# Four graph layers on one core: part of the first chunk's row sums moves from TensorE to VectorE, and the work between layers is put in another order

## The reference

```python
def gat(h, W, a):                       # layers 0 and 1; 2 and 3 have other ways to u, v
    Wh = h @ W
    e = leaky_relu((Wh @ a1)[:, None] + (Wh @ a2)[None, :], 0.2)
    att = softmax(where(adj > 0, e, -9e15), axis=1)
    return elu(att @ Wh)

h = relu(layernorm(x)); x = x + gat(h, W0, a0)
h = relu(layernorm(x)); x = x + gat(h, W1, a1)
h0 = relu(layernorm(x))
h1 = 0.2 * h0 + 0.8 * layer(h0, W2[0]); h2 = 0.2 * h0 + 0.8 * layer(h1, W2[1])
x = x + concat([h0, h1, h2]) @ mlp_w + mlp_b
h = relu(layernorm(x)); n = normalize(centre(h))
A = adj * softmax((n @ w_k) @ (n @ w_q).T / sqrt(8)); A = A / A.sum(-1)
x = x + (A + A @ A / 2 + A^4 / 6) @ h
```

## Time and profile before

| what | value |
|---|---|
| median of 3 runs | 585.03 us (584.64 to 595.99) |
| the profiled execution's own time | 580.28 us |
| its span, first to last instruction | 578.4 us |
| mean granted TensorE clock | 0.988 of full speed |
| TensorE busy | 529.5 us, 92% of the span |
| VectorE busy | 380.3 us, 66% |
| ScalarE busy | 263.3 us, 46% |

### The profile page before, as it was taken

The page is one execution under the profiler, slowest core; times in us unless marked ns, Lnnn a source line. Parts: engine busy times, 40 slices in busy tenths (PEclk is TensorE's granted clock), DMA queues, the critical chain, the costliest instruction groups (busy, mean ns, idle before and its releaser), DMA issues.

```text
span 578.4 us, 7918 instructions
## 1 busy us (share of the span) xinstructions
PE 529.5 (92%) x3300; PEld 202.4 (35%) x3300; DVE 380.3 (66%) x551; ACT 263.3 (46%) x297; POOL 30.2 (5%) x32
## 2 busy tenths in 40 slices
PE   6888987998998998998888999999889999999997
PEld 5422222343223343323233223245334344333332
DVE  4888689548979637989765989637977983100000
ACT  3479964534665543665543755444234772000000
POOL 3300000211000100000100000021100000000000
PEclk9879999999999999999999999999999999999999
DMA  8977000000000000000000000000000000000000
GB/s 309 409 280 275 4 1 1 0 2 1 1 0 1 2 0 2 1 1 0 1 1 2 0 2 1 0 1 1 1 1 1 0 1 2 0 1 1 0 19 18
DMA packets 5635, 19.43 MB, mean 34 GB/s; under 512 B 608, under 2 KB 608, under 8 KB 5600
## 3 DMA queue, kind: packets, MB, share of 16 engines
q1 hardware_dynamic: 5600, 18.93, 8.9%
HBM read 18.40 MB, written 0.52 MB: 33 GB/s over the span
## 4 chain that ended last, share of the span: by engine, by line
PE 63%; DVE 23%; ACT 6%; issue 4%; DMA 3%; POOL 1%; SPq 0%; DVEq 0%; ACTq 0%
PE PROD L793 11%; DVE X L1361 10%; PE X L1062 10%; PE PROD L1062 9%; PE X L785 7%; PE S L813 6%; ACT big L471 4%; DMA big<-in_adjT 3%; PE X L1053 2%; DVE tops L1625 2%; DVE big L1373 2%; PE M L648 1%; DVE nadj L1475 1%; PE M L747 1%; DVE big L1370 1%
## 5 line engine op out<-in xcount | busy, mean ns | idle before, releaser
L471 ACT ACTIVATE big<-X,v 128x1024 f32<-128x1024 f32 x128 | 141.6, 1114 | 100.5 <-PE X L785 100.1
L1361 DVE SCALAR_TENSOR_TENSOR X<-wB,v,aB 128x1024 f32<-128x1024 f32 x128 | 163.4, 1293 | 27.6 <-ACT big L471 26.3
L793 PE MATMUL PROD<-big,Wh 128*64 128x512 f32 x512 | 134.3, 605 | 1.9 <-ACT big L471 1.7
L785 PE MATMUL X<-nadj,bigI 128*64 128x512 bf16 x512 | 77.9, 383 | 19.6 <-DVE X L1361 19.3
L785 PEld LDWEIGHTS X<-nadj,bigI 128*64 128x64 bf16 x512 | 25.3, 109 | 102.3 <-DVE X L1361 73.2
L813 PE MATMUL S<-big,onesf 128*32 128x512 f32 x400 | 53.3, 604 | 2.4 <-DVE big L1373 2.4
L793 PEld LDWEIGHTS PROD<-big,Wh 128*64 128x64 f32 x512 | 31.1, 136 | 52.2 <-issue 30.3
L1062 PE MATMUL PROD<-big,Wh 128*64 128x512 f32 x128 | 30.6, 594 | 0.0
L528 ACT ACTIVATE big<-nadj 128x1024 fp8e4<-128x1024 bf16 x26 | 26.3, 1053 | 9.0 <-DVE nadj L1475 9.0
L398 POOL TENSOR_TENSOR rr<-var,mhalf 128x8 f32<-128x8 f32 x8 | 14.5, 1818 | 298.7 <-DVE var L1222 298.7
L1062 PE MATMUL X<-big,Wh 128*64 128x512 f32 x128 | 28.6, 595 | 0.0
(11 more groups left out here) (307 smaller groups left out, 597.2 us busy)
## 6 DMA issues: line engine op xcount, KB each, us to landing
big<-in_adjT SPq DMA_DIRECT2D x28, 512.0 KB, 7.5
aB<-in_adjT SPq DMA_DIRECT2D x4, 512.0 KB, 7.5
cst<-in_cst SPq DMA_DIRECT2D x1, 537.0 KB, 7.5
x<-in_xT SPq DMA_DIRECT2D x1, 512.0 KB, 3.7
out<-x SPq DMA_DIRECT2D x2, 256.0 KB, 2.0
late<-in_late SPq DMA_DIRECT2D x1, 272.5 KB, 5.8
cst<-in_cst SPq DMA_DIRECT2D x1, 263.0 KB, 2.8
```

The costliest lines, as they stand in the source:

```text
L471: act.activation(prob[:, t % U, :], X[t % 2][:], ACT.Exp, bias=v2[l % 2][:, k:k + 1]).then_inc(p_ready, 1)
L785: last = pe.matmul(X[t % 2][feat(side), hh * BANK:(hh + 1) * BANK], bigI[:, feat(side)], nadj[:, k, half_cols(c, hh)], start=False, stop=T ...
L793: last = pe.matmul(PROD[c][feat(hh), :], Wh[l % 2][:, k, :], prob[:, t % U, hh * BANK:(hh + 1) * BANK], start=k == 0, stop=k == NB - 1)
L1361: dve.scalar_tensor_tensor(X[t % 2][:], wB[:, cols(c)], v8[l % 2][:, k:k + 1], aB[:, cols(c)], ALU.max, ALU.add).then_inc(x_written, 1)
```

## The change

Six things change.

1. **First chunk.** `added(0)` is now (4, 5, 8, 9, 12). VectorE adds these tiles into h0, which is not yet used for its own purpose: 4 and 5 after the exponents of tile 7, 8 after tile 10, 9 after 11, 12 after 14. `sums` of the pairs (4, 5) and (8, 9) are not issued; the sums of (12, 13) read h0 in place of tile 12.
2. **Loads and early products.** Blocks 18 to 21 of `adj` go to slots 0 to 3, the others of the second half to other slots than before. Two `repeat` products each follow the level products of blocks 9, 10, 12 and 13; six in place of four follow `w_broadcast(1)`.
3. **End of the first chunk.** The level products of blocks 14 and 15 go ahead of the sums of tiles 10 and 11, and `shift_products(0, 2, 4)` goes ahead of the products of tiles 12 and 13. In the last pair the next chunk's masks go ahead of the sums.
4. **From layer 0 to 1 and from 1 to 2.** The first chunk's `features` on TensorE go from in front of the last sums to behind `centre`; on VectorE its features, rows, levels and row parts go behind `clip`. The early levels go behind all of this in one piece, and `w_broadcast` goes behind the next layer's top levels, in front of the shift products. In layer 2 `root_broadcast(0)` goes behind the shift products, and `input_rows(0)` on VectorE behind the exponents of tile 1.
5. **The terms of h0 and h1 in the `mlp`.** They leave `mlp(c)` for `skip_terms(c)`, into banks of their own: chunk 0 at the end of layer 2, chunk 1 at the start of layer 3, where 8 `repeat` products stand in place of 17. `skip_rows(c)` adds them and the bias to x; `mlp_rows` becomes a plain addition.
6. **From layer 2 to 3.** `features(7)` goes ahead of the last 20 early level products; three `repeat` products stand in place of four.

```diff
+        ADD_FIRST = {7: (5,), 10: (8,), 11: (9,), 14: (12,)}
         ADDS = 4
-        SLOT_OF = [n % SLOTS for n in range(NB)] + [(7, 8, 4, 5, 6)[j % 5] for j in range(NB)]
+        SLOT_OF = [n % SLOTS for n in range(NB)] + [(7, 8, 0, 1, 2, 3, 4, 5, 6, 7, 8, 4, 5, 6, 7, 8)[j] for j in range(NB)]
...
             if c_all == 0:
-                return ()
+                return (4, 5, 8, 9, 12)
...
+        def sum_buffer(c_all):
+            return acc[c_all % NCH] if c_all else h0[:].rearrange("p c n -> p (c n)")
...
+        def skip_bank(c):
+            return (X[1][:, BANK:CH], M[:])[c]
...
             def top_levels(l):
...
-                pe.wait_ge(wB_ready, 2 * (2 * l + 1))
+                if l in (0, 3):
+                    pe.wait_ge(wB_ready, 2 * (2 * l + 1))
                 for jb in range(CB if l else 0, NB):
                     if l == 0:
                         chunk_levels(0, jb)
+                        if jb in (9, 10, 12, 13):
+                            repeat(X[1][:, BANK:CH], 2)
                         continue
...
-                if l == 2:
-                    root_broadcast(0)
-                elif l:
+                if l in (1, 2):
+                    w_broadcast(2 * l)
+                if l:
                     repeat(X[0], 4)
...
                 shift_products(l, 0, 4 if l else 2)
+                if l == 2:
+                    root_broadcast(0)
...
             def mlp(c):
                 n = NCH * 3 + c
-                pe.wait_ge(ld_late, 16)
                 pe.wait_ge(p_copied, n + 1)
-                for k, src in enumerate((h0, h1)):
-                    pe.matmul(EB[c][:], mw[:, k, :], src[:, c, :], start=k == 0, stop=False)
                 pe.wait_ge(t_ready, n + 1)
-                pe.matmul(EB[c][:], mw[:, 2, :], tb, start=False, stop=False)
+                pe.matmul(EB[c][:], mw[:, 2, :], tb, start=True, stop=False)
...
+            def skip_terms(c):
+
+                pe.wait_ge(ld_late, 16)
+                pe.wait_ge(h0_ready, c + 1)
+                pe.wait_ge(h_ready, c + 1)
+                pe.matmul(skip_bank(c), mw[:, 0, :], h0[:, c, :], start=True, stop=False)
+                pe.matmul(skip_bank(c), mw[:, 1, :], h1[:, c, :], start=False, stop=True).then_inc(skip_psum, 1)
...
                 if l < 2:
                     centre_old(2 * l + 3)
-                    early_levels(l + 1, 0, 2)
                     centre(2 * l + 3)
-                    w_broadcast(2 * l + 2)
+                    features(2 * l + 2)
                     variances(2 * l + 3)
-                    early_levels(l + 1, 2, 4)
                     features(2 * l + 3)
-                    early_levels(l + 1, 4, CB)
                     repeat(X[0], 2)
+                    early_levels(l + 1, 0, CB)
+                    w_rows(2 * l + 2)
...
+            def skip_rows(c):
                 dve.wait_ge(ld_late, 16)
-                dve.wait_ge(mlp_psum, c + 1)
-                ins = dve.scalar_tensor_tensor(x[:, c, :], EB[c][:], mb, x[:, c, :], ALU.add, ALU.add)
-                signal(ins, x_new, 2 * 2 + c + 1)
+                dve.wait_ge(skip_psum, c + 1)
+                link(dve.scalar_tensor_tensor(x[:, c, :], skip_bank(c), mb, x[:, c, :], ALU.add, ALU.add))
```

More of the change, by code:

```diff
@@ L334, in by_dve @@
         def by_dve(n):
-            return n < NB and n % 3 == 0
+            return n % 3 == 0 if n < NB else False
         def copies_by_dve(n):
@@ L553, in _ @@
                     if l == 0 and k % 2 and k < 12:
-                        adjacency8(NB + 3 + k)
-                        adjacency8(NB + 4 + k)
+                        for n in (NB + 3 + k, NB + 4 + k):
+                            if not by_dve(n):
+                                adjacency8(n)
                     if l == 0 and k == 13:
@@ L776, in shift_products @@
                 for q in range(lo, hi):
+                    if l in (1, 2) and q == 2:
+                        pe.wait_ge(wB_ready, 2 * (2 * l + 1))
                     rows = slice(WIN * q, WIN * (q + 1))
@@ L808, in sums @@
                 if k - 1 in added(c_all):
-                    pe.wait_ge(p_added, ADDS * c_all)
+                    pe.wait_ge(p_added, ADDS * (c_all + 1))
                 for strip in range(4):
                     tile, hh = t - 1 + strip // 2, strip % 2
-                    src = acc[c] if tile == t - 1 and k - 1 in added(c_all) else prob[:, tile % U, :]
+                    src = sum_buffer(c_all) if tile == t - 1 and k - 1 in added(c_all) else prob[:, tile % U, :]
                     last = pe.matmul(S[32 * strip:32 * strip + 32, :], onesf[:, 0:32],
@@ L902, in _ @@
                 w_rows(2 * l + 1)
-                repeat(M, 17 if l else 8)
+                if l == 3:
+                    skip_terms(1)
+                    repeat(PROD[0], 8)
+                else:
+                    repeat(M, 17 if l else 8)
                 if l == 0:
@@ L907, in _ @@
                     w_broadcast(1)
-                    repeat(PROD[0], 4)
+                    repeat(PROD[0], 6)
                 pe.wait_ge(nv_ready, 4 * (l + 1) if l else 2)
@@ L926, in _ @@
                             products(0, 0, k + 1)
-                            if p == 6:
-                                shift_products(0, 2, 4)
-                            if p < NB // 2 - 1:
-                                mask(0, 0, k + 2)
-                                mask(0, 0, k + 3)
-                            sums(0, 0, k + 1)
-                            for jb in range(4 + k if p else 2, 6 + k if p < 6 else 0):
-                                chunk_levels(1, jb)
-                            if p == NB // 2 - 1:
-                                mask(0, 1, 0)
-                                mask(0, 1, 1)
+                            for i in range(2):
+                                if p < NB // 2 - 1:
+                                    mask(0, 0, k + 2 + i)
+                                else:
+                                    mask(0, 1, i)
+                            if p == 5:
+                                chunk_levels(1, NB - 2)
+                                chunk_levels(1, NB - 1)
+                            sums(0, 0, k + 1)
+                            for jb in range(4 + k if p else 2, 6 + k if p < 5 else 0):
+                                chunk_levels(1, jb)
+                            if p == 5:
+                                shift_products(0, 2, 4)
                             continue
@@ L1545, in _ @@
                             for n in range(NB + (5 if k > 1 else 4) + k, NB + 6 + (k if k else -1)):
-                                mask_words(n)
+                                convert(n)
+                        for i in ADD_FIRST.get(k, ()):
+                            accumulate(0, 0, i)
                         if k == 13:
@@ L1558, in _ @@
                     if k == 1 and l == 2:
+                        input_rows(0)
                         activated(1, 1)
+                    if k == 1 and l == 3:
+                        skip_rows(1)
                     if k == 11 and l == 2:
@@ L1615, in _ @@
                     activated(l, 1)
+                    skip_rows(0)
                 if l < 2:
                     clip(2 * l + 3)
+                    features(2 * l + 2)
                     variance(2 * l + 3)
+                    for i in range(2):
+                        feature_rows(2 * l + 2, i)
+                    block_levels(l + 1, 0, CB)
+                    row_parts(2 * l + 2)
                 if l < 3:
```

57 lines of the change are left out of this document (32 added, 25 removed).

## The result

The changed kernel takes 577.16 us (median of 4 runs, 575.72 to 577.80), the kernel before, timed beside it, 584.84. The profiled execution took 575.72 us with a span of 573.9, against 580.28 and 578.4 before. So the two traces differ by 4.5 us only, the medians by 7.7.

What follows compares the result with a forecast made beforehand. The chain of waits ran through TensorE for 63% and VectorE for 23%, all three engines near the bound in the first chunk. Terms sum to -5.6 from the 585.03 median: 579.4 us, likeliest 578 to 581, range 574.5 to 583.5.

Steps and rivals of the forecast that it cites:

- Clock ahead of the chunk: Ahead of the first chunk, eight `repeat` products keep TensorE at 2.4 GHz, so the shift starts sooner: -1.2 us.
- ScalarE's copies, which end last there: Ahead of the first chunk, the fillers wait for nothing and do not delay ScalarE's copies; part of the -1.2 us.
- First chunk: First chunk's exponents to the second's: two 1.0 us sums leave TensorE, four additions come to VectorE; -0.7, ends -3.1 to +3.4.
- The pair (4, 5) gains 0.5: First chunk: without its sums this pair gains 0.5 us and is then held by ScalarE.
- what the second missing sum and the earlier level products give: First chunk from tile 10: a gain that the additions of 8, 9 and 12 eat, all but 0.2 us.
- Layer 0 to 1, 1 to 2: Between these layers, reordered work comes earlier, but fillers and moved work take most back: -0.2 us each.
- The end of -0.9: Layers 0 to 1 and 1 to 2: far end of each -0.2 us term, if fillers don't hold the mask.
- Layer 2 to 3: Layer 2 to 3: `features(7)` follows earlier, top levels start at 307.35 instead of 308.29: -0.95 us.
- The two `mlp`: Layer 3: h0 and h1 terms leave the path, -1.8 us in chunk 0 and -0.55 in chunk 1.
- `skip_terms(0)` at nothing: End of layer 2: its two products of 0.9 us each fit into TensorE's idle 1.99 us ahead of 304.02.
- more comes through: Rival: first chunk goes as VectorE's work allows (-2.4 more) or two transitions give 0.9 each: 575.6 to 578; chance 0.2.
- The slower one: Rival: TensorE waits for VectorE in the first chunk and its clock falls; from two stretches on, 586.2 us; chance 0.05.

## Why the prediction came out as it did

Forecast 579.4, measured 577.2, inside the range.

- **Clock ahead of the chunk, -1.2.** Right for an execution like the one it was read from: -1.26 in the first traces, 1.33 with the fillers taken out. As a term for every execution it was too large. In the second trace of the kernel before the clock was full there, and the first exponents came at 41.65 against 41.70. The step that fails there is "ScalarE's copies, which end last there": TensorE, with the fillers in its list, ends last. How much of the 1.2 is in the median stays open. (That TensorE at 1.00 busy "holds full clock in the rows" is also misread: rows 2 have it 1.00 busy at a clock of 0.50.)
- **First chunk, -0.7.** Too large, and its parts were wrong. The stretch that the term speaks of became 0.27 shorter, not 0.7. Another 0.35 came in the second chunk, whose first exponential stands 2.01 behind its first exponents in place of 2.46, since its masks now go ahead of the sums; the forecast had no term for that, so it is luck that the two together make -0.6. "The pair (4, 5) gains 0.5" and "what the second missing sum and the earlier level products give" failed: the sums give nothing, the reordered end of the chunk gives 1.55, and the addition of tile 12 takes 1.14 of that. That the stretch ends in VectorE's work was right. The Trainium skill's Perfetto Trace Analysis, Identifying the Most-Contended Engine, takes the busy share as a measure of the limit for VectorE and ScalarE, and not for TensorE's matmuls. On this part the trace agrees with it, with 36.53 against 36.67: less work on TensorE gained nothing.
- **Layer 0 to 1, 1 to 2, -0.2 each.** Right (-0.21, -0.17), and by the reasons given: fillers and `w_broadcast` ahead of the shift products, 17 fillers ahead of the mask. The end of -0.9 "where fillers don't hold the mask" was too far for layer 2: with eleven of them VectorE holds the next tile.
- **Layer 2 to 3, -0.95.** Too large by 0.3, in size and not in mechanism. As forecast, TensorE's early levels and three `repeat` end last ahead of the top levels. But `features(7)` started 0.1 later than forecast, and from there to the top levels it took 3.04 us (302.88 to 305.92) in place of 2.9. One `repeat` instead of three gives 0.42.
- **The two `mlp`, -2.35.** -2.19 in the traces, 2.18 when undone.
- **`skip_terms(0)` at nothing.** This is the step that failed most, and with it the way from the trace to the median. "`skip_terms(0)` fits into TensorE's idle 1.99 us" put a cover for the clock at zero, because the one trace at hand showed no fall there. The second trace of the kernel before shows it, and filling the gap takes 1.4 us off the median; so "585.03 - 5.6" carried over a loss that the change removes: some 1.4 us of the 2.2 by which the forecast missed. The rest is within what one set of runs differs from the next (ratios 0.9867 and 0.9889). That the forecast came so near is in part luck: the marks gave 5.1 in place of 5.6, the start gave nothing in the second pair of traces, and the cover, put at nothing, made up for it. Whether the change also spares the fall in the last part is open, since it was seen in one trace of the kernel before and one of another.

The rival "more comes through" gave the right time, but neither of its mechanisms was at work. The slower one had no sign: clock 1.00 through the chunk. That "all terms at their far ends together" reach 573.3 doesn't add up: they make 9.4 us, which leaves 575.6.

## What to carry to other kernels

Place work that is moved to another engine by where that engine waits last: three of four additions were free and useless, the fourth stood behind the last wait and cost nearly its whole length (1.14 of 1.22 us). Idle time of the matrix engine is no free space: look at the granted clock behind each gap in more than one trace, and ask why the profiled run is faster than the median before a sum is made against it. Products issued only to hold the clock are themselves waited for; count them at each place.

## What the runs showed of the hardware

A gap of 1.99 us in TensorE's work at 302 to 304 us was followed by half clock in three of four traces, and each of these falls cost 1.58 to 2.65 us; with eight products of 0.24 us in the gap, or `skip_terms(0)`, none followed. In the load stage the clock is at half speed from 12 or 13 to 20 us in some traces and from 28 to 32 in others. With the new start and its fillers the first exponents come at 40.4 to 40.6 in four traces of the first kind and at 41.5 to 41.7 in four of the second, while later marks repeat to a few hundredths. With the old start the clock falls again ahead of the chunk in the first kind (34 to 40) and inside it in the second (45 to 49), where the stretch is 38.17 in place of 38.08.

GpSimd's `xq<-h` takes 1.11 us beside VectorE's addition `x<-big` and exponents (228.39 above), and 0.62 in the kernel with fewer fillers, where `activated` is gone from beside it; two exponents that begin beside it take 2.72 to 2.74 us in place of 2.49. The Trainium skill's SBUF — State Buffer, SBUF: two separate sides, says that a VectorE operation with two inputs from SBUF and one of GpSimd that reads SBUF lock each other out of a port pair that they share. The trace agrees.
